# The threshold search of a routed feed-forward: a loop over wide compares, or straight-line code with compares in four pieces

## The reference, cut to what matters

```
probs = softmax(layernorm(x) @ Wr + br)          # 2048 x 8
for every expert e:
    the 256 tokens with the highest probs[:, e], ties by position
    y = (silu(x @ W_up[e // 2] + b_up) @ W_down[e] + b_down) * probs
    out[tokens] += y
x = x + tanh(g_ffn[0]) * out
```

## Time and profile before

| what | us |
|---|---|
| three runs, median | 1974.95 |
| lowest and highest of them | 1974.83 and 1985.27 |
| span of the profiled execution, first to last instruction | 1977.2 |

### The profile page before, as it was taken

The page is one execution under the profiler, slowest core; times in us unless marked ns, Lnnn a source line. Parts: engine busy times, 40 slices in busy tenths (PEclk is TensorE's granted clock), DMA queues, the critical chain, the costliest instruction groups (busy, mean ns, idle before and its releaser), DMA issues.

```text
span 1977.2 us, 29280 instructions
## 1 busy us (share of the span) xinstructions
PE 1612.8 (82%) x10304; PEld 1214.1 (61%) x10305; DVE 1106.3 (56%) x2541; ACT 834.3 (42%) x1854; POOL 296.8 (15%) x351
## 2 busy tenths in 40 slices
PE   5899971795788875478887999999879873999997
PEld 3566660673555543345554778787645453999997
DVE  5666526413699998767654353535469966222221
ACT  3455430232676652345554522212369951322221
POOL 1100000442112000101110000000102201333332
PEclk8899975897799987689999999999979985999999
DMA  7445243125466231435525000000446625422221
GB/s 159 59 75 79 44 157 131 33 38 100 97 130 118 57 80 45 69 46 76 71 34 237 1 1 1 1 1 15 73 69 99 110 93 208 142 34 35 37 37 27
DMA packets 86653, 144.34 MB, mean 73 GB/s; under 512 B 14330, under 2 KB 70146, under 8 KB 83330
## 3 DMA queue, kind: packets, MB, share of 16 engines
q1 hardware_dynamic: 66562, 102.86, 22.3%
q0 software_dynamic: 19968, 39.87, 12.7%
HBM read 75.63 MB, written 27.79 MB: 52 GB/s over the span
## 4 chain that ended last, share of the span: by engine, by line
PE 56%; DVE 24%; ACT 7%; issue 6%; DMA 5%; SPq 1%; POOL 0%; DVEq 0%; POOLq 0%; ACTq 0%
PE ps L1361 12%; PE ps L1469 7%; PE ps L1480 7%; PE ps L1330 4%; DVE probs L2203 3%; DMA Qpack<-QP 3%; PE ps L1004 2%; PE ps L1241 2%; PE ps L861 2%; ACT pT L1605 2%; PE ps L1251 2%; PE ps L951 2%; PE ps L942 2%; PE ps L890 2%; PE ps L1386 2%
## 5 line engine op out<-in xcount | busy, mean ns | idle before, releaser
L345 POOL DMA_DIRECT2D Kpack<-KP x192 | 101.6, 537 | 969.0 <-PE ps L1361 381.8
L1600 ACT ACTIVATE pT<-ps 128x512 f32<-128x512 f32 x256 | 151.9, 607 | 185.0 <-PE ps L945 98.0
L942 PE MATMUL ps<-Qpack,Kpack 99*128 99x256 bf16 (+1 forms) x768 | 166.4, 283 | 19.7 <-ACT pT L1605 9.9
L1469 PEld LDWEIGHTS ps<-xgT,XNT 128*128 128x128 f32 x1280 | 151.4, 194 | 2.0
L1469 PE MATMUL ps<-xgT,XNT 128*128 128x128 f32 x1280 | 151.5, 277 | 0.0
L1480 PE MATMUL ps<-w,mid 128*128 x640 | 144.6, 379 | 0.0
L911 PE MATMUL ps<-Kpack,Qpack 97*128 97x256 bf16 x512 | 102.9, 287 | 40.4 <-DVE mx L2104 11.4
L1874 ACT ACTIVATE mid<-ps 128x512 f32<-128x512 f32 x80 | 43.4, 595 | 207.9 <-PE ps L1469 207.9
L1480 PEld LDWEIGHTS ps<-w,mid 128*128 128x128 f32 x640 | 118.6, 190 | 14.5
L1605 ACT ACTIVATE pT<-ps,nmax 128x256 f32<-128x256 f32 x256 | 121.6, 557 | 10.9 <-DVE nmax L2116 10.7
L2104 DVE CUSTOM_DVE_ANT_0 Vb<-ps,mask_bf 128x256 bf16<-128x256 f32 x256 | 94.8, 419 | 52.2 <-PE ps L911 52.1
(11 more groups left out here) (309 smaller groups left out, 3308.3 us busy)
## 6 DMA issues: line engine op xcount, KB each, us to landing
Kpack<-KP POOLq DMA_DIRECT2D x192, 128.0 KB, 5.0
Qpack<-QP SPq DMA_DIRECT2D x192, 128.0 KB, 6.3
w<-in_w SPq DMA_DIRECT2D x16, 1024.0 KB, 6.3
ctxT<-in_ctxT SPq DMA_DIRECT2D x32, 256.0 KB, 7.9
h_rows<-in_h SPq DMA_DIRECT2D x16, 512.0 KB, 7.2
h<-h_rows SPq DMA_DIRECT2D x2, 4096.0 KB, 22.7
wd<-in_wd SPq DMA_DIRECT2D x4, 1536.0 KB, 14.9
xn_rows<-xn SPq DMA_DIRECT2D x16, 256.0 KB, 2.4
```

What stands on the lines that cost most here:

```text
L345: eng.dma_start(Kpack[j][DH * k:DH * (k + 1)].rearrange("d (e f) t -> d e (f t)", f=HALF), KP[par][:, part]).then_inc(done, 16)
L942: mm = pe.matmul(A[h % ring][:, t], Kpack[par][0:rows, h, t * P:(t + 1) * P], Qpack[par][0:rows, h], start=True, stop=L != 0)
L1469: mm = pe.matmul(bank[:, f % 4 * P:(f % 4 + 1) * P], w1_tile[k % 2][:, c, f * P:(f + 1) * P], xgT3[k % 2][:, c], start=c == 0, stop=c == K ...
L1600: act.activation(pT[h % 8][:], A[h % 2][:], ACT.Exp).then_inc(s["exp_done"], 1)
```

## The change

The hardware loops on DVE and PE are gone: the ten digits are written out. The big compare of a digit is four compares of four token tiles each (224 numbers), each with an increment of `thr_cmp` of its own. PE waits for each piece and counts it with four matmuls of 56 columns, one per token tile; all 16 of a digit are summed in one accumulator of 56 columns, so that the reduction `cnt` is gone. The steps of all ten digits are made once, by POOL, at the head of its `ffn0`; the rescaling and the conversion in each digit are gone. The next candidates are made in two parts: `near` = threshold OR next steps, made while PE counts, and `cand` = `near` OR `taken`, made at the head of the digit. The update of the threshold moves behind the compares.

```diff
-DIGIT_BITS, DIGITS, UNROLL0 = 3, 10, 2
-COUNTED0 = 4
+DIGIT_BITS, DIGITS = 3, 10
+PIECES0 = 4
+PIECE0 = NT // PIECES0
...
+            def digit_steps():
+                pool.iota(step_i[:, DIGITS - 1], pattern=[[1, DIGIT]], base=1, channel_multiplier=0).then_inc(s["steps_ready"], 1)
+                pool.wait_ge(s["steps_ready"], 1)
+                pool.tensor_copy(step_f[:, DIGITS - 1], step_i[:, DIGITS - 1]).then_inc(s["steps_ready"], 1)
+                pool.wait_ge(s["steps_ready"], 2)
+                for r in range(DIGITS - 1):
+                    e = pool.tensor_scalar(step_f[:, r], step_f[:, DIGITS - 1], 2.0 ** (DIGIT_BITS * (DIGITS - 1 - r)), None, ALU.mult)
+                e.then_inc(s["steps_ready"], 1)
+                pool.wait_ge(s["steps_ready"], 3)
+                pool.tensor_copy(step_i[:, 0:DIGITS - 1], step_f[:, 0:DIGITS - 1]).then_inc(s["steps_ready"], 1)
+
             def ffn0(n):
+                digit_steps()
                 rows_sent(n)
...
             def ffn0(n):
-                with pe.Fori(0, DIGITS // UNROLL0) as i:
-                    for d in range(UNROLL0):
-                        pe.wait_ge(s["thr_cmp"], UNROLL0 * i + d + 1)
-                        for t in range(0, NT, COUNTED0):
-                            mm = pe.matmul(ps[1][:].rearrange("p a b -> p (a b)")[:, 0:DIGIT * COUNTED0 * E0], ones_bf[:],
-                                           above[:, :, t:t + COUNTED0], start=t == 0, stop=t + COUNTED0 == NT)
-                        mm.then_inc(s["thr_cnt"], 1)
-
-                pe.wait_ge(s["thr_cmp"], DIGITS + 1)
+                for d in range(DIGITS):
+                    for t in range(NT):
+                        if t % PIECE0 == 0:
+                            pe.wait_ge(s["thr_cmp"], PIECES0 * d + t // PIECE0 + 1)
+                        mm = pe.matmul(ps[1][:, 0, 0:DIGIT * E0], ones_bf[:], above[:, :, t], start=t == 0, stop=t == NT - 1)
+                    mm.then_inc(s["thr_cnt"], 1)
+
+                pe.wait_ge(s["thr_cmp"], PIECES0 * DIGITS + 1)
                 counts(0, ps[2], 2 * NT * E0)
...
                 dve.memset(thr[:], 0)
-                for j in range(DIGIT):
-                    dve.memset(step_f[:, j], (j + 1) * 2.0 ** (DIGIT_BITS * (DIGITS - 1)))
-                    dve.memset(step_i[:, j], (j + 1) << (DIGIT_BITS * (DIGITS - 1)))
+                dve.memset(taken[:], 0)
+                dve.wait_ge(s["steps_ready"], 4)
+                wide = [P, DIGIT, E0]
+                dve.tensor_copy(near[:], step_i[:, 0].unsqueeze(2).to_broadcast(wide))
                 chain(1, dve.tensor_tensor(probs_e[:], route[1][:], bc_row(row_m[:, 2]), ALU.mult))
...
+                of_e = [P, DIGIT, PIECE0, E0]
+                counted = ps[1][:, 0, 0:DIGIT * E0].rearrange("p (j e) -> p j e", e=E0)
+                for d in range(DIGITS):
+                    k = 1 + 4 * d
+                    chain(k + 1, dve.tensor_tensor(cand[:], near[:], taken[:].unsqueeze(1).to_broadcast(wide), ALU.bitwise_or))
+                    for t in range(0, NT, PIECE0):
+                        dve.tensor_tensor(above[:, :, t:t + PIECE0], probs_e[:, t:t + PIECE0].unsqueeze(1).to_broadcast(of_e),
+                                          cand[:].bitcast(F32).unsqueeze(2).to_broadcast(of_e), ALU.is_ge).then_inc(s["thr_cmp"], 1)
+                    chain(k + 2, dve.tensor_tensor(thr[:], thr[:], taken[:], ALU.bitwise_or))
+                    if d + 1 < DIGITS:
+                        dve.tensor_tensor(near[:], step_i[:, d + 1].unsqueeze(2).to_broadcast(wide), thr[:].unsqueeze(1).to_broadcast(wide), ALU.bitwise_or)
+                    dve.wait_ge(s["thr_cnt"], d + 1)
+                    chain(k + 3, dve.scalar_tensor_tensor(reached[:], counted, TOP0 - 0.5, step_f[:, d].unsqueeze(2).to_broadcast(wide), ALU.is_ge, ALU.mult))
+                    chain(k + 4, dve.tensor_reduce(taken[:], reached[:].rearrange("p j e -> p e j"), AX.X, ALU.max))
+                k = 1 + 4 * DIGITS
+                chain(k + 1, dve.tensor_tensor(thr[:], thr[:], taken[:], ALU.bitwise_or))
+                k += 1
```

More of the change, by code:

```diff
@@ L223, in program @@
         cand = sb("cand", [P, DIGIT, E0], I32, f0c)
-        step_i = sb("step_i", [P, DIGIT, E0], I32, f0c)
-        step_f = sb("step_f", [P, DIGIT, E0], F32, f0c)
+        near = sb("near", [P, DIGIT, E0], I32, f0c)
+        step_i = sb("step_i", [P, DIGITS, DIGIT], I32, f0c)
+        step_f = sb("step_f", [P, DIGITS, DIGIT], F32, f0c)
         reached = sb("reached", [P, DIGIT, E0], F32, f0c)
         taken = sb("taken", [P, E0], I32, f0c)
-        cnt = sb("cnt", [P, DIGIT, E0], F32, f0c)
         above = sb("above", [P, DIGIT, NT, E0], BF16, f0c)
@@ L310, in program @@
                  "nmax_ready rsum_ready vs_ready sc1_ps sc1_done m1_step m1_ready sum1_step norm1 av1_done x_ffn "
-                 "pack_const pack_rows rt_const rt_logits rt_step rt_exp rt_cnt rt_prefix thr_step thr_cmp thr_cnt "
+                 "pack_const pack_rows rt_const rt_logits rt_step rt_exp rt_cnt rt_prefix steps_ready thr_step thr_cmp thr_cnt "
                  "xn_out0 xn_out1 xn_out2 xn_out3 rows_ready "
@@ L2440, in route0 @@
-                k = 1 + 6 * DIGITS
+                of_e = [P, DIGIT, PIECE0, E0]
[12 more added lines that the diff above has]
+                    chain(k + 4, dve.tensor_reduce(taken[:], reached[:].rearrange("p j e -> p e j"), AX.X, ALU.max))
```

## The result

| | kernel before | changed kernel |
|---|---|---|
| median of six runs, us | 1976.40 | 1963.41 |
| span of the profiled execution, us | 1977.2 | 1961.2 |
| first `cand` to flags, us | 38.87 | 25.77 |

The ratio of the times is 0.9924, with a 95% interval of 0.9901 to 0.9948: 15.0 us less, between 10.3 and 19.6. The medians themselves differ by 13.0. One of the six runs of the changed kernel, of 3948.62 us, was a disturbed one and is not in the ratio.

The account below looks back on a forecast made before the run. Bound by latency, DVE and PE taking turns: a digit falls from 3.72 to 2.54 us, the search from 38.87 to 25.6 (-13.3), entry -0.2. In all 13.5 us off the median 1974.95 gives 1961.5 us, range 1958 to 1968.

Parts of the forecast that it names:

- A stretch bound by latency, with no cover: Search from first `cand` to flags, 38.87 us: DVE and PE wait in turn, so every step saved comes off the end.
- Compares in pieces: DVE in each digit: four compares of 224 numbers start 0.31 us apart, 1.32 in place of 1.09, +0.23.
- The non-overlapping compares: Rival, chance 0.10: compare pieces on DVE run end to end, 0.42 us apart, 3.3 us more in all, 1964.8.
- Narrow matmuls: PE in each digit: only the last four 56-column matmuls count, 0.35 us in place of 0.93, -0.58.
- its weight load: Rival, chance 0.07: the sixteen matmuls of a digit start 0.132 us apart, a digit is 3.46, the time 1970.7.
- a floor: Rival, chance 0.04: each narrow counting matmul is as slow as one of 224 columns, 0.18 us apart, the time 1979.6.
- The reduction goes: DVE in each digit: `cnt` and its gap vanish, -0.43 us; `reached` reading PSUM instead of SBUF costs nothing.
- The preparation is hidden, by 0.10: DVE behind a digit's last compare: `thr` and `near` end at 0.73 us, PE's result comes at 0.83.
- The loop: Hardware loop in the search: each turn's branch costs 0.38 us, so writing out the digits saves 1.5 over four turns.
- The entry: Ahead of the first `cand`: fourteen presets go, a copy and a preset come, 0.46 us in place of 0.68, -0.2.
- Straight-line code comes late: Rival, chance 0.07: instruction stall, in the search or a later stage, like 4.94 us ahead of the router; time 1966.4.
- The clock rises early: Rival, chance 0.04: TensorE's clock goes from 0.50 to 1.00 in the search, `up` wins up to 2.0 us; 1958.5.

Follow-up runs that it names:

- the two comparisons of whole runs: The changed kernel against the kernel before, measured twice: ratio 0.9924 first, then 0.9933 with the changed kernel run once more, medians 1968.30 and 1978.17 us.

## Why the prediction was right

The forecast was 13.5 us less; the stretch itself gave 13.35, and the two comparisons of whole runs 15.0 and 13.3 by the ratio, 13.0 and 9.9 by the medians. The stretch is what confirms the sum; whole runs agree with it but are too wide to test it. That the forecast time of 1961.5 lies 1.9 from the measured 1963.41 is in part luck: it stands on the median of three runs, 1974.95, and six gave 1976.40, while single undisturbed runs of the changed kernel lie between 1961.18 and 1968.06. By the steps of the prediction:

- *A stretch bound by latency, with no cover.* Right: from the first `cand` to the first `up` it was 361.52 - 298.69 = 62.83 us and is 343.47 - 293.63 = 49.84, 12.99 less, so nearly all of the 13.10 that the search gave up arrives there.
- *Compares in pieces,* 0.31 apart and 1.32 together. Measured 0.305 and 1.30. The non-overlapping compares (a digit of 2.87) are excluded. The section of the Trainium skill that the prediction names for them (VectorE: DVE Perf Modes, "The DRAIN you can't avoid") adds that an instruction that isn't held starts earlier, which the prediction left out. The compares agree with that: 0.305 apart where one lasts 0.384.
- *Narrow matmuls,* 0.045 apart and 0.22 long, 0.35 for the last four. Measured 0.047 and 0.228, so 0.37. This was the term with the widest bounds and no row of its width; 0.8 ns a column, from 224 columns, held at 56. Both rivals that made a matmul dearer, by its weight load or by a floor, are excluded by the kernel with one piece.
- *The reduction goes,* -0.43: 0.42 by the kernel that keeps it. `reached` from PSUM lasts 0.218, as long as from SBUF, and from its start to that of `taken` it is 0.26 from PSUM in the changed kernel and 0.25 from SBUF in the one that keeps the reduction. The estimate from the Trainium skill's table of fixed costs (VectorE: DVE Perf Modes, "The TRN2 errata"), 0.065 more a digit, does not hold here.
- *The preparation is hidden, by 0.10.* It is, by 0.13.
- *The loop,* -1.5 for four turns: 1.6 with the exit.
- *The entry,* 0.46: 0.43. *POOL's table,* 3 us at 204: 3.3 us at 202.
- *Straight-line code comes late*: not in the search, whose digits are even to 0.02 us in every kernel with the loops written out. The 4.94 us ahead of the router, which I took for an example of such a stall, are none. In the kernel before:

```profile
274.39 2.78 DVE L2002 TENSOR_SCALAR xn<-X,ln_tmp 128x256 f32 x8 [0.63 <-DVE ln_tmp L1963]
...
275.23 2.79 PE L796 MATMUL ps<-ident,xn 128*128 128x128 f32 x12 [4.94 <-issue]
```

PE's transposes read `xn`, and DVE and ScalarE are at the layer norm until DVE starts to write `xn` at 274.39; two tiles of it are there by about 275.1. The chain calls the wait "issue" because it names nothing that released it; the kernel has one, the semaphore `xn_ready`. The changed kernel has the same 4.94. Among the later stages the longest wait so named is 11.58 us in the kernel before and 12.13 in the changed one.
- *The clock rises early*: it did not, and it did not either in the kernel that adds two matmuls to every digit, with PE busy 16.63 of 20 us. The gain of 2 us that I priced at the first `up` is real, and came where ten wide matmuls ran right ahead of it.

The digit came out within 0.01 us, with two terms off by 0.02 in opposite directions: the compares took 1.30 instead of 1.32, the last four matmuls 0.37 instead of 0.35.

Two statements of what would be seen were off: the flags at 324 us and `up` at 348. They came at 319.4 and 343.5, because I gave times from the span's start, and the start of the search itself moves by 8.6 us from execution to execution. A distance from the first `cand` would have been the right thing to name.

Open is what makes TensorE's clock around the router differ from one execution to the next, and what makes the time behind the first `up` differ by up to 15.6 us; no kernel here was made to test it.

## What to carry to other kernels

Where two engines take turns, write down one turn from the timeline, start to start, until the pieces add up to the measured distance; then each edit is a difference of rows, and here a sum of eight terms came out within 0.01 us a digit. Cut a producer's work so that the consumer's last piece is small, but count the start of every piece: here the optimum was flat and soon reached, and three unequal pieces with a small last one (2.43 us a digit) were better than four or eight equal ones (2.55 and 2.73). Where whole runs scatter by more than the gain, judge the variants by the length of their own stretch.

## What the runs showed of the hardware

TensorE's clock stayed at 0.50 (1.2 GHz) through 20 us in which PE was busy 16.63 us with gaps of 0.42 us. In two kernels it rose to 1.00 (2.4 GHz) with ten gapless matmuls of 512 columns in bf16 ahead, and the first `up` took 5.42 us in both. In the router of the kernel before PE was busy without a gap too, with transposes and matmuls in f32, and the clock stayed at 0.50:

```profile
284.00:291.00 7.00, 7.00 (x36) 7.00 (x36) 0.00 (x0) 1.77 (x3) 0.00 (x0) 0.50 0.95 383
```

Why one rose and the other did not is not shown. Ten otherwise useless instructions shortened the work up to the second `up` by some 2 us.

A matmul of 56 columns in bf16, with its weights loaded anew each time, starts 0.047 us after the last at the lower clock; the load's own 0.12 us is hidden.

Compares on VectorE without a wait between them overlap: 224 numbers last 0.384 us and start 0.305 apart. A PSUM input cost `reached` at most 0.01 us more than an SBUF one.
